# Experts in which a chunk's products stand ahead of the next chunk's transposes, and a different place for the first expert's preparation on GpSimd

## The reference

```python
x = _layernorm(x + self_attention(x))
x = _layernorm(x + cross_attention(x, ctx_1024))          # x2 in the kernel
logits = einsum('bsd,ed->bse', x, gate_w)
scores = softmax(logits, -1).transpose(0, 2, 1)
topk_w, topk_idx = top_k(scores, cap)                     # cap = 32 rows of each sequence for each of 16 experts
x_tok = take_along_axis(x[:, None], topk_idx[..., None], 2)
g = einsum('becd,efd->becf', x_tok, Wg)                   # 256 -> 512
u = einsum('becd,efd->becf', x_tok, Wu)                   # 256 -> 512
h = gelu(g) * u
eo = einsum('becf,edf->becd', h, Wd) * topk_w[..., None]  # 512 -> 256
# eo is added back at topk_idx, plus the shared feed-forward, plus x; then a layer norm
```

## Time and profile before

| | us |
|---|---|
| median of 3 runs | 3325.5 (3321.42 to 3326.87) |
| the profiled execution's own time | 3324.87 |
| its span, first to last instruction | 3323.1 |
| TensorE busy in the span | 3182.9 (96%) |
| VectorE, ScalarE, GpSimd busy | 2349.3, 2197.2, 1391.2 |

### The profile page before, as it was taken

How to read it: one execution, slowest core, us unless ns; L and a number is a source line. 1 busy time by engine, 2 the same in 40 slices (tenths; PEclk the granted TensorE clock), 3 DMA queues, 4 the chain that set the end, 5 groups by cost and what they waited for, 6 DMA issues and landing times. The chain is left out here.

```text
span 3323.1 us, 80850 instructions
## 1 busy us (share of the span) xinstructions
PE 3182.9 (96%) x23456; PEld 3000.1 (90%) x23456; DVE 2349.3 (71%) x6770; ACT 2197.2 (66%) x7067; POOL 1391.2 (42%) x2767
## 2 busy tenths in 40 slices
PE   5999999999999968999999999999599999989999
PEld 4999999999999958999999999999488888879999
DVE  5777777777777756777878777788454544537777
ACT  5878788787787857777777777778244444424433
POOL 3666766676766653333333333333422322200000
PEclk8999999999999979999999999999799999999999
DMA  5444444444444420010100001011233333224433
GB/s 174 111 115 127 126 122 118 125 112 120 127 123 123 112 93 17 23 33 24 35 25 27 30 27 33 23 33 36 75 96 114 99 97 113 95 67 121 123 118 103
DMA packets 201355, 283.79 MB, mean 85 GB/s; under 512 B 33344, under 2 KB 149952, under 8 KB 200384
## 3 DMA queue, kind: packets, MB, share of 16 engines
q1 hardware_dynamic: 194880, 262.91, 27.7%
q0 software_dynamic: 6144, 16.79, 1.6%
HBM read 124.41 MB, written 41.94 MB: 50 GB/s over the span
## 5 line engine op out<-in xcount | busy, mean ns | idle before, releaser
L863 POOL TENSOR_SCALAR ca_prob<-ca_prob,ca_inverse 128x120 f32<-128x120 f32 x1024 | 354.4, 365 | 649.7 <-DVE ca_inverse L1179 647.7
L603 ACT ACTIVATE sa_prob<-sa_prob,sa_shift 128x128 f32<-128x128 f32 (+1 forms) x1024 | 453.3, 460 | 7.4 <-DVE sa_shift L644 6.0
L1107 ACT ACTIVATE ca_prob<-bank,ca_shift 128x120 f32<-128x120 f32 x1024 | 355.2, 370 | 5.0 <-DVE ca_shift L1173 4.3
L644 DVE CUSTOM_DVE_ANT_0 sa_prob<-bank,sa_mask 128x128 f32<-128x128 f32 (+1 forms) x1024 | 304.6, 352 | 8.9 <-issue 5.2
L1401 POOL DMA_INDIRECT first_x_raw<-mid_x,ex_tokens x124 | 163.7, 1320 | 344.4 <-PE bank L1417 312.4
L411 POOL TENSOR_SCALAR sa_prob<-sa_prob,sa_inverse 128x128 f32<-128x128 f32 x512 | 197.1, 385 | 244.4 <-DVE sa_inverse L652 230.1
L131 PE MATMUL bank<-sa_ow,sa_y_hi 128*128 128x256 f32 x1024 | 278.1, 303 | 0.0
L131 PE MATMUL bank<-sa_kvT_a,sa_q 128*128 128x128 f32 (+1 forms) x1024 | 254.3, 285 | 22.4 <-DMA sa_q<-sa_q_tile 17.3
L133 PE MATMUL bank<-sa_kvT_b,sa_q 112*128 112x128 f32 (+1 forms) x1024 | 261.8, 281 | 0.0
L675 DVE TENSOR_TENSOR sa_pT_lo<-bank,sa_pT_hi 128x384 fp32r<-128x384 f32 x512 | 258.0, 543 | 0.6 <-ACT sa_pT_hi L590 0.6
L133 PE MATMUL bank<-sa_ow,sa_y_lo 112*128 112x256 f32 x1024 | 257.1, 283 | 0.0
(11 more groups left out here) (265 smaller groups left out, 12264.4 us busy)
## 6 DMA issues: line engine op xcount, KB each, us to landing
sa_q<-sa_q_tile SPq DMA_DIRECT2D x128, 288.0 KB
sa_q<-sa_q_tile SPq DMA_DIRECT2D x160, 112.0 KB
mid_eo<-ex_out SPq DMA_DIRECT2D x32, 512.0 KB, 3.0
co_eo_raw<-mid_eo SPq DMA_DIRECT2D x128, 128.0 KB, 2.7
sa_q<-sa_q_tile SPq DMA_DIRECT2D x304, 32.0 KB
sa_xT_raw<-in_xT SPq DMA_DIRECT2D x32, 256.0 KB, 3.1
sa_q<-sa_q_tile SPq DMA_DIRECT2D x32, 256.0 KB
sa_x_res<-in_x SPq DMA_DIRECT2D x32, 256.0 KB, 3.0
```

What stands on the lines that cost most here:

```text
L603: act.activation(prob[:, r, hh, cols], prob[:, r, hh, cols], ACT.Exp, bias=shift[:, r, n:n + 1], scale=-1.0, accum_out=total[:, r, n:n + 1 ...
L644: dve.tensor_tensor_reduce(out=prob[:, r, hh, cols], in0=SC[hh][:, t * T:t * T + (t + 1) * P], in1=mask[:].rearrange("p a s -> p (a s)")[: ...
L863: ins = pool.tensor_scalar(prob[:, r, t, hh], prob[:, r, t, hh], inverse[:, r, n:n + 1], 1.0, ALU.mult, ALU.mult)
L1107: act.activation(prob[:, r, t, hh], SC[g % 2][:, n * S:n * S + S], ACT.Exp, bias=shift[:, r, n:n + 1], accum_out=total[:, r, n:n + 1]).the ...
```

## The change

Two things. In the cross-attention stage, three step numbers: the hi split of the first expert's weights goes from step 5 to step 4, the lo split from step 11 to step 5, the 4 gathers from step 2 to step 8. In the experts, on TensorE, ScalarE and VectorE alike, the part for chunk m now stands behind the part for chunk m - GL instead of ahead of it. SyncE and GpSimd keep their order there. No instruction is added or taken away.

```diff
-        X0_IN, W0_HI, W0_LO = 2, 5, 11
+        W0_HI, W0_LO, X0_IN = 4, 5, 8
...
         def _(pe):
             def body(J):
                 for m in range(XBODY):
-                    n = m
-                    if exists(J, n):
-                        i = n % 2
-                        need(pe, x_in[i], J * (8 * XBODY * TILES) + 16 * TILES * (n // 2 + 1))
-                        need(pe, xlo_done, n_of(J, n - 1))
-                        for k in range(KC):
-                            for t in range(TILES):
-                                mm = pe.transpose(XT[k][:, t * P:t * P + P], x_raw[:, i, t, k * P:k * P + P], ident[:])
-                        mm.then_inc(x_tr, 1)
                     n = m - GL
                     if exists(J, n):
...
                             mm.then_inc(u_mm, 1)
+                    n = m
+                    if exists(J, n):
+                        i = n % 2
+                        need(pe, x_in[i], J * (8 * XBODY * TILES) + 16 * TILES * (n // 2 + 1))
+                        need(pe, xlo_done, n_of(J, n - 1))
+                        for k in range(KC):
+                            for t in range(TILES):
+                                mm = pe.transpose(XT[k][:, t * P:t * P + P], x_raw[:, i, t, k * P:k * P + P], ident[:])
+                        mm.then_inc(x_tr, 1)
                     n = m - DL
...
```

More of the change, by code:

```diff
@@ L1460, in body @@
                 for m in range(XBODY):
+                    n = m - GL
+                    if exists(J, n):
+                        i = n % 2
+                        need(act, d_mm, n_of(J, n - 2, 2))
+                        for f in range(FT + 1):
+                            if f < FT:
+                                need(act, g_mm, n_of(J, n, FT, f - FT + 1))
+                                need(act, hid_done, n_of(J, n, FT, f - FT - 1))
+                                act.activation(act_g[:, f % 2], GB[f % 2][:], ACT.Gelu).then_inc(gelu_done, 1)
+                            if f > 0:
+                                need(act, hid_done, n_of(J, n, FT, f - FT))
+                                act.activation(h_hi[:, i, f - 1], hid[:, (f - 1) % 2], ACT.Copy).then_inc(hhi_done, 1)
                     n = m
@@ L1476, in body @@
                         ins.then_inc(xhi_done, 1)
[L1477 to L1488, removed]
                     n = m - DL
@@ L1501, in body @@
                 for m in range(XBODY):
+                    n = m - GL
+                    if exists(J, n):
+                        i = n % 2
+                        for f in range(FT + 1):
+                            if f < FT:
+                                need(dve, u_mm, n_of(J, n, FT, f - FT + 1))
+                                need(dve, gelu_done, n_of(J, n, FT, f - FT + 1))
+                                need(dve, hhi_done, n_of(J, n, FT, f - FT - 1))
+                                need(dve, hlo_done, n_of(J, n, FT, f - FT - 1))
+                                dve.tensor_tensor(hid[:, f % 2], act_g[:, f % 2], UB[f % 2][:], ALU.mult).then_inc(hid_done, 1)
+                            if f > 0:
+                                need(dve, hhi_done, n_of(J, n, FT, f - FT))
+                                dve.tensor_tensor(h_lo[:, i, f - 1], hid[:, (f - 1) % 2], f32(h_hi[:, i, f - 1]),
+                                                  ALU.subtract).then_inc(hlo_done, 1)
                     n = m
@@ L1515, in body @@
                         ins.then_inc(xlo_done, 1)
[L1516 to L1529, removed]
                     n = m - DL
```

## The result

The changed kernel takes 3355.1 us (median of 6 runs, 3350.36 to 3362.89) against 3322.6 us before (6 runs, 3320.89 to 3326.87): a ratio of 1.0099, 95% interval 1.0083 to 1.0114. It is 32.5 us slower. The forecast was 3353. The profiled execution took 3361.38 us, one of the slowest of the six.

The account below looks back on a forecast made before the run. It took TensorE, busy in 96% of the span, as the bound. 27.3 + 0.8 - 3.6 + 0.8 - 4.2 = +21.1 us, with the clock +27.9; 3324.9 + 27.9 = 3352.8, forecast 3353, range 3339 to 3369 us.

Parts of the forecast that it names:

- the signs named for it: In the experts: about 15 waits of 2.2 to 2.4 us on `x_lo`, none on `hid`, granted clock below 0.99.
- The chain against one D: Experts' first chunks: splits end T (GU's end) + 8.84, next GU due T + 6.45; +27.3 us, 14 experts.
- Chunk 3: In the experts, this chunk has the three shared splits ahead of its own split: +0.8 us.
- The start: Start of the experts: GU(0) no longer waits for chunk 1's gathers, -8.5 us, partly given back: -3.6 us.
- The last steps of cross-attention: Softmax rows no longer wait behind the gathers; GpSimd's queue is late next: -4.2 us, bounds 0 and -7.
- The clock: Experts: four of 16 waits above 2 us followed by a low stretch: +6.8 us, bounds 0 and 27.
- The rival in which nearly every wait brings a fall: Experts: the clock falls after every long wait, 27 us in place of 6.8, giving 3373 us; chance 0.13.
- The sum: Whole kernel: +21.1 us without clock falls, +27.9 with them, added to the profiled execution's 3324.9 us.

Follow-up runs that it names:

- half a chain: Changed kernel with only the gate and up columns of each expert's weights split ahead of the chunk's split, down columns behind it: 3321.2 us, 0.9999.
- the pair with the waits filled: Changed kernel with ten discarded matmuls in each expert's wait from the second on, with the new step numbers (3346.0 us) and with the old (3350.3 us).
- the pair that ran side by side: Changed kernel timed again (3352.4 us) beside the changed kernel with ten discarded matmuls per expert's wait from the second on (3346.0 us).
- the kernel that splits a chunk earlier: Changed kernel with the next expert's gate and up columns split behind the second chunk's own split, down columns behind the first chunk's split: 3310.9 us, 0.9964.

## Why the prediction was right

The mechanism was the one foreseen, and the signs named for it came: 14 waits of 2.45 us on `x_lo`, none on `hid`, the splits of `ahead_w` 76.5 us apart (foreseen 74 to 77), 2.9 us of waiting behind GU(0), a granted clock of 0.97 from 2374 to 2985 us. The terms one by one:

- *The chain against one D.* Right, in place and nearly in size. Foreseen T + 8.84, measured 8.94; foreseen a loss of 1.95 us net for each expert. Where no low stretch fell, the transposes of two neighbouring experts' first chunks were 37.62 us apart (2712.53 to 2900.63 for five experts) against 70.9 / 2 = 35.43, so 2.19, or 30.6 for 14 instead of 27.3. Of the 0.24 for each expert the chain itself explains 0.1; the rest stays open. The kernel with half a chain and the one with the weights' split put back show that it is this chain and nothing else of the new order.
- *Chunk 3.* Foreseen 0.8, the wait was 0.88.
- *The start.* Foreseen -3.6, with the fall behind the wait of GU(1) counted under the clock. The profiles give 43.1 - 45.3 = -2.2 with one such fall in it, so about -3.5 without. The parts hold too: GU(0) came 12.95 us behind the first transposes before and comes 4.53 behind them now, 8.4 less (foreseen 8.5), and the wait of GU(1) was 2.9 (foreseen 3.1).
- *The last steps of cross-attention.* Foreseen: the power from 2346.1 to 2346.8, normalization in 0.92; seen: from 2346.45 to 2347.18, and 0.73. The power was thus 0.4 later than foreseen, in an execution that was 1.15 later ahead of these steps. The sum of -4.2 stands against 4.0 in the profiles as they are, 5.2 counted from the last-but-one power, 2.6 in the medians of the kernel with the steps alone and 4.3 in the pair with the waits filled. Which engine is late next (GpSimd's queue) was right, and the kernel with the lo split behind the last normalization shows it.
- *The clock.* Foreseen four falls, 6.8 us, with a range to 27. The profiled execution had 8, and the pair that ran side by side says 6.4 us in the median. Of the 39.5 us that 14 experts took longer, 30.6 and the 0.9 of chunk 3 are the waits; the 8.0 left over make 1.3 for each of the six low stretches in them, where 1.7 was foreseen. Some of the stretches began within the wait, where TensorE loses nothing. Four was a guess between bounds, and that its sum comes close to the median is partly luck. One of the two examples it started from was also weaker than it was read: the clock had been at the low level ahead of that wait of 2.45 us too, until 1245 us (0.50 in the window 1243 to 1245).
- *The rival in which nearly every wait brings a fall* did not come about: 8 of 16 in one of the slowest executions, 6 in the changed kernel's other profile, 3 in that of the kernel with the new order alone.
- *The spread.* The number of falls differs from run to run. It fits that the changed kernel spreads over 13 us and the one with the waits filled over 3 to 5, but falls were counted in profiled executions only, and the kernel that splits a chunk earlier spreads over 12 us with no fall in its experts behind GU(1). So the falls are not the only cause of spread.
- *The sum.* Without the clock 21.1 us were foreseen; the kernel with the waits filled is 24.6 slower than before (3346.0 - 3321.4), and most of the 3.5 between them is the 3.3 of the chain. With the clock 27.9 were foreseen and 32.5 measured, 31.0 the second time (3352.4 - 3321.4). That 3353 lies within 2 us of 3355.1 is partly luck: it was added to the profiled execution's 3324.9, and the kernel before had a median of 3322.6 beside the changed one, 2.3 less.

## What to carry to other kernels

When a stage is moved in a software pipeline, ask of each engine what now stands between the moved work and its first user, and count everything that is queued with it: here a small split (2.4 us) could move without cost, but the large one that only happened to stand in the same block (6.1 us more) could not. Repeated waits of TensorE can cost more than their length: of those of 2.45 us here some were followed by a stretch at the low clock, of those of 0.3 to 0.9 us none. When one job leaves the critical queue and another is put in its place, look at the time when the next input is ready; the gain stops there.

## What was not expected of the hardware

After waits of the same length (2.45 us, the same work on both sides), the clock fell after some and not after others, at times within the wait and at times 1.5 us behind it; the wait of GU(1) was followed by a fall in one profile of a kernel and not in another of the same kernel. In the kernel with half a chain, waits of 0.3 to 0.9 us brought no fall within the experts. Ten idle matmuls in each wait kept the clock up (1.00 over 566 us) and saved 6.4 us.
